# A scan, a sorted mixture of experts and a gated feed-forward on one core: x takes the normalisation's bias ahead of the chain, the down product goes in pieces, and the order tables are new

## The chip, the cores and the metric

The kernel runs on one NeuronCore of a Trainium2 chip. A core has a matrix engine (TensorE, PE in the rows; its weight loads are PEld), a vector engine (VectorE, DVE), an activation engine (ScalarE, ACT), a general engine (GpSimd, POOL) and a queue that mostly starts transfers (SyncE, SP). Each runs its own instruction stream in the order in which it is written; they meet only at semaphores. The metric is the device time of one execution in microseconds (us). Before the change it is 979.82 us, the median of three runs (976.91 to 981.39).

## The reference

The input x is (8, 1024, 128) in f32: 8 sequences of 1024 tokens with 128 features.

```python
def step(h, inps):                                   # over the tokens of a sequence; h is (batch, 128, 16)
    x_t, d_t, B_t, C_t = inps                        # d = softplus(x Wd + bd), B = x WB + bB, C = x WC + bC
    bar_A = jnp.exp(jnp.minimum(d_t[:, :, None] * A, 2.0))           # A = -exp(A_log)
    bar_B = jnp.clip(d_t[:, :, None] * B_t[:, None, :], -2.0, 2.0)
    h = jnp.clip(bar_A * h + bar_B * x_t[:, :, None], -100.0, 100.0)
    return h, jnp.sum(h * C_t[:, None, :], axis=-1) + x_t * D_param
...
routing = softmax(flat @ Wr + br);  top1_w, top1_i = max, argmax     # flat: the scan's outputs, 4 experts
hid = silu(flat @ up_w[e] + up_b[e]);  all_out = hid @ down_w[e] + down_b[e]      # hidden size 512
out = ssm_out + sel * top1_w                                         # sel: the output of the chosen expert
attn = (out - mu) * rsqrt(var + EPS) * ln_w + ln_b
...
x = _layernorm(x + attn)
x = _layernorm(x + (silu(x wg) * (x wu)) wd)         # hidden size 384, weights are integers times 1/127
```

So there are three normalisations over the 128 features: the first (k = 0 in the code) has the weight `ln_w` and the bias `ln_b`, the second (k = 1) follows after x has been added, the third (k = 2) comes after the feed-forward.

## The kernel before, in words

A chunk is one sequence; there are 8. Each is handled whole (1024 tokens, in two halves of 512 where a PSUM bank asks for it, and in 8 tiles of 128 tokens). The stages of a chunk:

- **Inputs of the scan**: TensorE's products z and bc, ScalarE's softplus, VectorE's `delta` (L966) and `dx` (L971), a split of B into three bf16 parts (`bc_rest` on GpSimd L1166, `bc_mid`, `bc_low`), and a bound (`bound_input`, `bound`, `over`, `flag`) which shows whether any clipping can matter; if none can, the scan takes the fast branch.
- **The scan**: 16 states s. For each, ScalarE makes the decay (L758), TensorE spreads row s of B over 128 partitions (`spread`, L519, into psB, one buffer), VectorE multiplies by dx (L1124) and scans in two halves (L1133, three state buffers), GpSimd multiplies by C (`prod`, L1160, three buffers), and TensorE adds the product, turned, into psY (`add`, L525).
- **The router and the sort**: y_copy, turn, logits, then on VectorE `router_shift` (L1004 to L1019), TensorE's `rank`, and VectorE's `slots` (L1037 to L1067). GpSimd scatters the 8 tiles to sorted rows in DRAM (`scatter`, L1181); SyncE reads them back as up to 11 blocks of 128 rows, each with one expert.
- **The experts**: per block a turn (`sort_turn`, `sort_copy`), `up` (L636), `silu` (L796), `down` (L652), `result` (L803), with the block's weights fetched by SyncE (512 KB each, three buffers: block k waits for result k-3). Results go to DRAM (`store`) and come back in token order (`gather` on GpSimd, L1189).
- **The rest**, by halves h: `combine` (VectorE, L1075: chosen output times weight plus y), `stats` k (L1092, L1097), `rstd` k (GpSimd, four tiny instructions L1198 to L1206), `norm` k (ScalarE, L815). Between the first and the second normalisation stands `affine` (GpSimd, L1217 to L1225), three instructions of 128x512: times `ln_w`, plus `ln_b`, plus x. Then x is turned and split in two parts (`x_turn` L661, `x_high`, `x_rest`, `x_low`), six up products `ff_up` (L677, L678), ScalarE's `gate` (L845), VectorE's `ff_mul` (L1104), `ff_down` (L688, L691), the third normalisation, and the output's transfer.

Nothing decides at run time which stage goes next. Five tables (`PE_ORDER`, `ACT_ORDER`, `DVE_ORDER`, `POOL_ORDER`, `SP_ORDER`) each list one round of an engine; an entry `(-1, "up", 3)` means "in round i, task up 3 of chunk i-1". So while chunk n is scanned, the experts of chunk n-1 and the feed-forward of chunk n-2 run beside it. A table can be cut at another point of the round without any change of order, so that only the relative order of entries counts. An engine that waits at one entry holds up all that follow it. The banks U0, U1, D and T of PSUM are counted by fills and drains in the order of `PE_ORDER`.

Since the line numbers move with the change, `affine` is at L1228 and L1234 after it, the products at L1166, the scatters at L1187, the decays at L764, and so on.

## Time and profile before

| what | value |
|---|---|
| runs | 976.91, 979.82, 981.39 us |
| profiled execution, own time | 977.01 us |
| its span, first to last instruction | 975.0 us |
| mean granted clock of TensorE | 0.824 |
| PE / DVE / POOL / ACT busy | 687.9 / 705.7 / 612.3 / 501.3 us |
| a full round (scan 15 to scan 15, chunks 3 to 6) | 102 to 105 us |
| after the last scan (821 to 975) | 154 us |

A timeline row reads: start in us from the span's beginning, duration in us, engine, line, operation, what is written and read, shape, count, and in brackets the idle time before it with what ended that idle time. Busy time on an engine is no proof that the engine sets the pace: with tables like these one reads round by round who waits for whom.

### The profile page before, as it was taken

The numbers are of one execution on the slowest core, as the hardware profiler recorded it, in microseconds if no ns is written. First come the engines' busy times: TensorE is split into PE (matmuls) and PEld (weight loads), VectorE is DVE, ScalarE is ACT, GpSimd is POOL, SyncE is SP. The second block draws the span as 40 slices with busy tenths as digits, with TensorE's granted clock in tenths as the row PEclk, the third lists the DMA queues.
The fourth block names the chain that finished last, engine by engine and source line by source line (L and its number), as shares of the span: only waits on it lengthen the run. The fifth ranks groups of instructions, "written<-read, shape, count | busy, mean of one in ns | idle before, by whom it ended". The sixth has DMA issues, their size and how long they took to land.

```text
span 975.0 us, 14730 instructions
## 1 busy us (share of the span) xinstructions
PE 687.9 (71%) x4648; PEld 549.3 (56%) x4648; DVE 705.7 (72%) x1330; ACT 501.3 (51%) x776; POOL 612.3 (63%) x516
## 2 busy tenths in 40 slices
PE   3465747884899579865997499838985798179244
PEld 1233526762687459743985288626873597158233
DVE  3699999789878988698868977898789764311131
ACT  5563354374664747384739474746643463054222
POOL 0376446468864889388948795689648874550540
PEclk8676877996799779985999599967996699579667
DMA  3333435844485527553765367444845373235100
GB/s 118 108 133 108 144 119 173 278 145 146 144 251 169 189 87 232 198 166 109 239 196 174 124 217 240 145 143 136 262 153 180 108 246 115 89 94 180 41 1 22
DMA packets 82086, 149.17 MB, mean 153 GB/s; under 512 B 9404, under 2 KB 51132, under 8 KB 81992
## 3 DMA queue, kind: packets, MB, share of 16 engines
q1 hardware_dynamic: 69192, 134.97, 42.6%
q0 software_dynamic: 4096, 8.40, 2.6%
q10 hardware_dynamic: 8704, 4.72, 1.8%
q8 instruction: 38, 0.62, 0.3%
q14 instruction: 56, 0.46, 0.2%
HBM read 132.64 MB, written 15.40 MB: 152 GB/s over the span
## 4 chain that ended last, share of the span: by engine, by line
PE 28%; POOL 22%; DVE 19%; issue 16%; ACT 6%; DMA 5%; SPq 1%; POOLq 0%; DVEq 0%; ACTq 0%
DVE state L1133 9%; POOL prod L1160 8%; PE psU L636 5%; DMA weights<-in_w_pack 4%; PE psT L652 4%; POOL rstd L1203 4%; PE psD L691 3%; PE psY L525 3%; DVE moe L1075 3%; POOL rows_in L1181 3%; PE psU L677 2%; DVE psB L1124 2%; PE psB L519 2%; PE psU L678 2%; DVE bst L1092 1%
## 5 line engine op out<-in xcount | busy, mean ns | idle before, releaser
L1160 POOL TENSOR_TENSOR prod<-state,c_wide 128x1024 f32<-128x1024 f32 x128 | 312.2, 2444 | 174.6 <-DVE state L1133 156.9
L519 PE MATMUL psB<-parts,sel 128*128 128x512 bf16 x256 | 110.4, 447 | 146.1 <-DVE state L1133 141.8
L1124 DVE TENSOR_TENSOR psB<-dx,psB 128x512 f32<-128x512 f32 x256 | 167.4, 689 | 34.3 <-PE psB L519 26.3
L1133 DVE TENSOR_TENSOR_SCAN state<-decay,state,psB 128x512 f32<-128x512 f32 x128 | 163.8, 1280 | 14.4 <-DVE state L1133 0.5
L525 PE MATMUL psY<-ident,prod 128*128 128x128 f32 x1024 | 157.9, 308 | 12.4 <-POOL prod L1160 12.4
L1133 DVE TENSOR_TENSOR_SCAN state<-decay,psB 128x512 f32<-128x512 f32 x128 | 155.2, 1213 | 5.1 <-ACT decay L758 4.8
L758 ACT ACTIVATE decay<-delta,a_sb 128x1024 f32<-128x1024 f32 x128 | 140.5, 1141 | 32.8 <-DVE state L1133 27.0
L525 PEld LDWEIGHTS psY<-ident,prod 128*128 128x128 f32 x1024 | 137.5, 160 | 28.7 <-POOL prod L1160 17.1
L519 PEld LDWEIGHTS psB<-parts,sel 128*128 128x128 bf16 x256 | 25.7, 103 | 201.5 <-DVE state L1133 190.3
L636 PE MATMUL psU<-yT_sorted,weights 128*128 128x128 f32 x704 | 126.0, 300 | 8.8 <-DMA weights<-in_w_pack 8.0
L636 PEld LDWEIGHTS psU<-yT_sorted,weights 128*128 128x128 f32 x704 | 111.0, 195 | 17.2 <-DMA weights<-in_w_pack 10.6
L796 ACT ACTIVATE hid<-psU 128x512 f32<-128x512 f32 x88 | 52.3, 594 | 103.3 <-PE psU L638 101.2
L652 PE MATMUL psT<-weights,hid 128*128 128x128 f32 x704 | 97.6, 282 | 0.0
L652 PEld LDWEIGHTS psT<-weights,hid 128*128 128x128 f32 x704 | 85.8, 192 | 1.3
L1181 POOL DMA_INDIRECT rows_in<-ytok,slot x64 | 66.7, 1043 | 30.8 <-issue 26.8
L1104 DVE SCALAR_TENSOR_TENSOR hh<-psU,hh 128x512 f32<-128x512 f32 x48 | 32.4, 689 | 70.9 <-PE psU L678 70.6
L638 PE MATMUL psU<-of_block,bias 96*128 96x128 bf16 x352 | 78.5, 223 | 0.0
L1189 POOL DMA_INDIRECT chosen_out<-rows_out,slot x64 | 61.7, 964 | 23.0 <-issue 14.6
L815 ACT ACTIVATE attn<-attn,shift,rstd 128x128 f32<-128x128 f32 x64 | 26.3, 482 | 70.1 <-POOL shift L1206 70.1
L815 ACT ACTIVATE moe<-moe,shift,rstd 128x128 f32<-128x128 f32 x64 | 26.3, 482 | 63.5 <-POOL shift L1206 63.0
L691 PE MATMUL psD<-wdn_sb,hh 128*128 128x128 f32 x384 | 53.3, 275 | 0.0
L1203 POOL TENSOR_TENSOR rstd<-ve,minus_half 128x4 f32<-128x4 f32 x48 | 49.2, 1025 | 3.8
(153 smaller groups left out, 1150.7 us busy)
## 6 DMA issues: line engine op xcount, KB each, us to landing
c_wide<-c_rows SPq DMA_DIRECT2D x128, 512.0 KB
weights<-in_w_pack SPq DMA_DIRECT2D x88, 512.0 KB, 4.7
xT_sb<-in_xT SPq DMA_DIRECT2D x8, 512.0 KB, 3.6
y_sorted<-rows_in SPq DMA_DIRECT2D x16, 256.0 KB, 3.0
xt<-in_x SPq DMA_DIRECT2D x8, 512.0 KB, 4.7
rows_out<-result SPq DMA_DIRECT2D x16, 256.0 KB, 5.5
out<-x ACTq DMA_DIRECT2D x16, 256.0 KB, 4.0
y_sorted<-rows_in SPq DMA_DIRECT2D x8, 192.0 KB, 4.8
```

The costliest lines, as they stand in the source:

```text
L519: pe.matmul(tokens(psB, c, h), sel[:, s, :], parts[:, c.n % 2, h * HALF:h * HALF + c.hw], start=True, stop=True).then_inc(b_ready, 1)
L525: mm = pe.matmul(psY[:, j, :], src[:, j * ROWS:(j + 1) * ROWS], ident[:, :], is_transpose=True, start=(first and j % NJ == 0), stop=last, ...
L636: pe.matmul(bank[u][:, cols], weights[:, q % NW, f * 128:(f + 1) * 128], yT_sorted[:, k * ROWS:(k + 1) * ROWS], start=(f == 0), stop=False ...
L638: mm = pe.matmul(bank[u][:, cols], bias3[:, f * 128:(f + 1) * 128], of_block[:, n % 2, k:k + 1].to_broadcast([96, ROWS]), start=False, sto ...
L652: mm = pe.matmul(bank[d][:, 0:D], hid[:, k % 2, f, :], weights[:, q % NW, W_DOWN + f * D:W_DOWN + (f + 1) * D], start=False, stop=(f == NF ...
L691: mm = pe.matmul(bank["D"][:, cols], hh[:, m, cols], wdn_sb[:, m, :], start=False, stop=(m == NH - 1), skip_group_check=True)
L758: nc.scalar.activation(decay[:, g % NDECAY, w], delta[:, n % 2, w], ACT.Exp, scale=a_sb[:, s:s + 1]).then_inc(decay_ready, 1)
L1124: v.tensor_tensor(tokens(psB, c, h), dx[:, n % 2, h * HALF:h * HALF + c.hw], tokens(psB, c, h), ALU.mult).then_inc(inp_ready, 1)
L1133: v.tensor_tensor_scan(state[:, g % NSTATE, t0:t0 + c.hw], decay[:, g % NDECAY, t0:t0 + c.hw], tokens(psB, c, h), before, ALU.mult, ALU.ad ...
L1160: g_.tensor_tensor(prod[:, g % NPROD, w], state[:, g % NSTATE, w], c_wide[:, g % NC, w], ALU.mult).then_inc(prod_ready, 1)
L1181: g_.indirect_dma_start(rows_in, bass.IndirectOffsetOnAxis(slot[:, n % 2, j:j + 1].bitcast(U32), 0), ytok[:, n % 2, j, :], None).then_inc( ...
L1203: g_.tensor_tensor(rstd[:, h, hj], ve[:, h, hj], minus_half[:, hj], ALU.pow).then_inc(rstd_steps, 1)
```

## The change

Four edits:

1. `affine` loses its middle instruction. A new task `x_shift` on GpSimd adds `ln_b` to x in place, as soon as x has come in; `affine` is then times `ln_w`, plus the shifted x. The semaphore counts go from 3 to 2 a turn, and `affine` waits for `shifted`.
2. `ff_down` keeps only the products with the identity (x into the bank); three new tasks `ff_part h m` add the hidden parts m = 0, 1, 2, each with its own wait for its `ff_mul`. Before, one task waited for all three and went tile by tile.
3. New tables for all five engines.
4. The tables are cut at other points of the round (which by itself moves nothing).

```diff
 PE_ORDER = [
...
+    (-1, "up", 3), (-2, "ff_down", 0), (-2, "ff_part", 0, 0), (-2, "ff_part", 0, 1), (-2, "ff_part", 0, 2),
...
 DVE_ORDER = [
-    (0, "router_shift"), (1, "scan", 3), (1, "scan", 4), (0, "slots"), (-1, "combine", 0), (-1, "stats", 0, 0),
+    (1, "scan", 2), (0, "router_shift"), (1, "scan", 3), (0, "slots"), (-1, "combine", 0), (-1, "stats", 0, 0),
...
 SP_ORDER = [
-    (-1, "c", 12), (-2, "weights", 5), (-1, "c", 13), (-2, "weights", 6), (-1, "c", 14), (-2, "weights", 7),
+    (-3, "weights", 5), (-3, "weights", 6), (-2, "c", 13), (-3, "weights", 7), (-2, "c", 14), (-3, "weights", 8),
...
+            def add_ff(c, h, m):
+                u = f"U{(m + NH) % 2}"
+                pe.wait_ge(drained[u], fills(u, c, ("ff_up", h, m + NH)))
+                for j in range(c.hj):
+                    cols = slice(j * 128, (j + 1) * 128)
+                    mm = pe.matmul(bank["D"][:, cols], hh[:, m, cols], wdn_sb[:, m, :], start=False,
+                                   stop=(m == NH - 1), skip_group_check=True)
+                if m == NH - 1:
+                    mm.then_inc(filled["D"], 1)
...
                 if name == "ff_down":
                     (h,) = args
-                    for m in range(NH):
-                        u = f"U{(m + NH) % 2}"
-                        pe.wait_ge(drained[u], fills(u, c, ("ff_up", h, m + NH)))
                     fill("D", c, task)
                     for j in range(c.hj):
-                        cols = slice(j * 128, (j + 1) * 128)
-                        pe.matmul(bank["D"][:, cols], ident127[:, :], attn[:, h * NJ + j, :], start=(j == 0), stop=False,
-                                  skip_group_check=True)
-                        for m in range(NH):
-                            mm = pe.matmul(bank["D"][:, cols], hh[:, m, cols], wdn_sb[:, m, :], start=False,
-                                           stop=(m == NH - 1), skip_group_check=True)
-                    mm.then_inc(filled["D"], 1)
+                        pe.matmul(bank["D"][:, j * 128:(j + 1) * 128], ident127[:, :], attn[:, h * NJ + j, :],
+                                  start=(j == 0), stop=False, skip_group_check=True)
...
+                if name == "x_shift":
+                    (h,) = args
+                    jj = slice(h * NJ, h * NJ + c.hj)
+                    if n == 0 and h == 0:
+                        pool.wait_ge(consts_in, 16 * LATE)
+                    pool.wait_ge(xt_in, 16 * (n + 1))
+                    lb = lnb_sb[:, :].rearrange("p (o d) -> p o d", o=1).to_broadcast([128, c.hj, D])
+                    g_.tensor_tensor(xt[:, jj, :], xt[:, jj, :], lb, ALU.add).then_inc(shifted[h], 1)
                 if name == "affine":
...
                     g_.tensor_tensor(moe[:, jj, :], moe[:, jj, :], lw, ALU.mult).then_inc(affine_steps[h], 1)
-                    pool.wait_ge(affine_steps[h], 3 * turn + 1)
-                    g_.tensor_tensor(moe[:, jj, :], moe[:, jj, :], lb, ALU.add).then_inc(affine_steps[h], 1)
-                    pool.wait_ge(affine_steps[h], 3 * turn + 2)
-                    pool.wait_ge(xt_in, 16 * (n + 1))
+                    pool.wait_ge(affine_steps[h], 2 * turn + 1)
+                    pool.wait_ge(shifted[h], turn + 1)
```

What the new tables move, at three places. First GpSimd, from the product of scan 3 to that of scan 4 and beyond, with the first normalisation of half 0 (`ve` to `shift` is `rstd 0 0`). Before:

```order
L1160 TENSOR_TENSOR prod<-state,c_wide 128x1024
L1181 DMA rows_in<-ytok,slot 1408x128
L1160 TENSOR_TENSOR prod<-state,c_wide 128x1024
L1198 TENSOR_TENSOR ve<-mv,eps 128x4
L1200 TENSOR_TENSOR minus_mean<-mv,minus_one 128x4
L1203 TENSOR_TENSOR rstd<-ve,minus_half 128x4
L1205 ISA
L1206 TENSOR_TENSOR shift<-minus_mean,rstd 128x4
L1181 DMA rows_in<-ytok,slot 1408x128
L1217 TENSOR_TENSOR moe<-moe,lnw_sb 128x512
L1219 TENSOR_TENSOR moe<-moe,lnb_sb 128x512
L1225 TENSOR_TENSOR attn<-moe,xt 128x512
```

With the change:

```order
L1166 TENSOR_TENSOR prod<-state,c_wide 128x1024
L1204 TENSOR_TENSOR ve<-mv,eps 128x4
L1206 TENSOR_TENSOR minus_mean<-mv,minus_one 128x4
L1209 TENSOR_TENSOR rstd<-ve,minus_half 128x4
L1211 ISA
L1212 TENSOR_TENSOR shift<-minus_mean,rstd 128x4
L1221 TENSOR_TENSOR xt<-xt,lnb_sb 128x512
L1187 DMA rows_in<-ytok,slot 1408x128
L1166 TENSOR_TENSOR prod<-state,c_wide 128x1024
L1228 TENSOR_TENSOR moe<-moe,lnw_sb 128x512
L1234 TENSOR_TENSOR attn<-moe,xt 128x512
L1195 DMA chosen_out<-rows_out,slot 128x128
```

The reciprocal deviation now comes before the product of scan 4, the shift of x and a scatter stand between it and `affine`, and one gather has moved behind `affine`.

Second, GpSimd from the last six scatters on. Before:

```order
L1181 DMA rows_in<-ytok,slot 1408x128 x6
L1160 TENSOR_TENSOR prod<-state,c_wide 128x1024
L1166 TENSOR_TENSOR bnd<-bcf,parts 128x1024
L1198 TENSOR_TENSOR ve<-mv,eps 128x4
L1200 TENSOR_TENSOR minus_mean<-mv,minus_one 128x4
L1203 TENSOR_TENSOR rstd<-ve,minus_half 128x4
L1205 ISA
L1206 TENSOR_TENSOR shift<-minus_mean,rstd 128x4
L1160 TENSOR_TENSOR prod<-state,c_wide 128x1024
L1217 TENSOR_TENSOR moe<-moe,lnw_sb 128x512
```

With the change:

```order
L1187 DMA rows_in<-ytok,slot 1408x128 x6
L1221 TENSOR_TENSOR xt<-xt,lnb_sb 128x512
L1204 TENSOR_TENSOR ve<-mv,eps 128x4
L1206 TENSOR_TENSOR minus_mean<-mv,minus_one 128x4
L1209 TENSOR_TENSOR rstd<-ve,minus_half 128x4
L1211 ISA
L1212 TENSOR_TENSOR shift<-minus_mean,rstd 128x4
L1166 TENSOR_TENSOR prod<-state,c_wide 128x1024 x2
L1172 TENSOR_TENSOR bnd<-bcf,parts 128x1024
```

The product of scan 6 (`prod`, the first after the scatters) now stands behind the second shift of x and behind `rstd 1 0`; `bc_rest` (`bnd<-bcf,parts`) stands one product later.

Third, ScalarE from the split of x (`x1h`, `x1l`) to the first expert blocks (`ex` is the router's exponential, `hh` the gates, `yT_sorted` is `sort_copy 0`, `hid` is `silu`). Before:

```order
L832 ACTIVATE x1h<-psD 128x512
L758 ACTIVATE decay<-delta,a_sb 128x1024
L838 ACTIVATE x1l<-psD 128x512
L758 ACTIVATE decay<-delta,a_sb 128x1024
L780 ACTIVATE ex<-rs 128x32
L845 ACT_TABLE_LOAD
L845 ACTIVATE hh<-psU 128x512 x3
L787 ACTIVATE yT_sorted<-psD 128x512
L815 ACTIVATE moe<-moe,shift,rstd 128x128 x4
L796 ACTIVATE hid<-psU 128x512
```

With the change:

```order
L838 ACTIVATE x1h<-psD 128x512
L844 ACTIVATE x1l<-psD 128x512
L764 ACTIVATE decay<-delta,a_sb 128x1024
L851 ACT_TABLE_LOAD
L851 ACTIVATE hh<-psU 128x512 x3
L786 ACT_TABLE_LOAD
L786 ACTIVATE ex<-rs 128x32
L821 ACTIVATE moe<-moe,shift,rstd 128x128 x4
L764 ACTIVATE decay<-delta,a_sb 128x1024
L793 ACTIVATE yT_sorted<-psD 128x512
L802 ACT_TABLE_LOAD
L802 ACTIVATE hid<-psU 128x512 x2
```

The exponential has gone behind the gates, the normalisation `moe` (`norm 1 0`) and one decay ahead of `sort_copy 0`, and there are two more table loads. Over the whole kernel ScalarE has 58 table loads in place of 46.

Moves that are told in words: on VectorE `slots`, `combine 0` and `stats 0 0` come after scan 3 instead of scan 4, `router_pick` from after scan 1 to between the `ff_mul` of half 0, `delta` from behind scan 8 and `stats 1 0` to right behind scan 7, ahead of `combine 1`, `dx` from after scan 13 to after scan 12, `stats 1 1` and `stats 0 2` together after scan 11. On TensorE `yT_turn` comes right after z and ahead of the spread of scan 2, `up 3` ahead of `ff_down 0`, `down 8` behind the spread of scan 15. On SyncE weights 6 and 7 each move ahead of one load of C, the stores 0 and 1 after the next round's first load of C, and `over` behind weights 10. On ScalarE the third normalisation `norm 1 2` goes ahead of `y_copy`.

## Rows read from the trace of the kernel before

**Rows 1.** the page: span, and busy time of each engine with its share
```profile
span 975.0 us, 14730 instructions
...
PE 687.9 (71%) x4648; PEld 549.3 (56%) x4648; DVE 705.7 (72%) x1330; ACT 501.3 (51%) x776; POOL 612.3 (63%) x516
```

**Rows 2.** stretches: length; PE, PEld, DVE, ACT, POOL busy us; granted clock, DMA, GB/s
```profile
513.20:617.00 103.80, 83.26 (x595) 68.13 (x594) 85.47 (x164) 63.86 (x99) 78.81 (x65) 0.87 0.56 180
...
821.00:975.00 154.00, 79.15 (x506) 63.48 (x505) 30.55 (x145) 48.05 (x105) 59.78 (x85) 0.74 0.23 71
...
534.00:563.00 29.00, 14.84 (x52) 9.55 (x53) 26.29 (x62) 15.20 (x22) 23.69 (x23) 0.53 0.34 117
...
563.00:616.00 53.00, 50.02 (x409) 44.77 (x408) 40.49 (x75) 29.04 (x52) 37.63 (x31) 1.00 0.67 210
```

**Rows 3.** timeline, VectorE: start, us, instruction, [idle before]; flag of two chunks
```profile
301.00 0.64 DVE L994 TENSOR_REDUCE clip_flag<-over_row 1x1 int32<-1x512 f32 x1
...
714.92 0.64 DVE L994 TENSOR_REDUCE clip_flag<-over_row 1x1 int32<-1x512 f32 x1
```

**Rows 4.** timeline, VectorE then GpSimd: the two combines, and a product beside the first
```profile
536.03 4.14 DVE L1075 SCALAR_TENSOR_TENSOR moe<-chosen_out,top_w,ytok 128x128 f32<-128x128 f32 x4
...
554.34 1.12 DVE L1075 SCALAR_TENSOR_TENSOR moe<-chosen_out,top_w,ytok 128x128 f32<-128x128 f32 x4
...
537.66 2.35 POOL L1160 TENSOR_TENSOR prod<-state,c_wide 128x1024 f32<-128x1024 f32 x1
```

**Rows 5.** one line's instructions, VectorE: ns min/median/max; a timeline row of the second
```profile
L1075 DVE SCALAR_TENSOR_TENSOR moe<-chosen_out,top_w,ytok x64: 322/346/3261, 223.8 to 930.4; 128x128 f32<-128x128 f32 x64
...
L966 DVE SCALAR_TENSOR_TENSOR delta<-zb,sp x8: 1192/1212/7559, 16.9 to 663.6; 128x1024 f32<-128x1024 f32 x8
...
663.57 6.13 DVE L966 SCALAR_TENSOR_TENSOR delta<-zb,sp 128x1024 f32<-128x1024 f32 x1
```

**Rows 6.** groups by line, GpSimd; then its timeline at the scatters
```profile
L1219 POOL TENSOR_TENSOR moe<-moe,lnb_sb 128x512 f32<-128x512 f32 x16 | 20.3, 1270 | 1.3
...
560.42 1.97 POOL L1181 DMA_INDIRECT rows_in<-ytok,slot  x1 [0.30 <-issue]
...
562.42 2.39 POOL L1160 TENSOR_TENSOR prod<-state,c_wide 128x1024 f32<-128x1024 f32 x1
```

**Rows 7.** timeline, ScalarE then TensorE: second normalisation, first expert block
```profile
553.39 1.65 ACT L815 ACTIVATE attn<-attn,shift,rstd 128x128 f32<-128x128 f32 x4 [7.15 <-POOL shift L1206]
...
566.49 0.66 PE L624 MATMUL psD<-ident,y_sorted 128*128 128x128 f32 x4 [1.18 <-DMA y_sorted<-rows_in]
...
567.92 0.46 PE L636 MATMUL psU<-yT_sorted,weights 128*128 128x128 f32 x2
```

**Rows 8.** timeline, VectorE: its waits in a round
```profile
571.23 0.69 DVE L1124 TENSOR_TENSOR psB<-dx,psB 128x512 f32<-128x512 f32 x1 [1.24 <-POOL prod L1160]
...
599.71 0.06 DVE L984 MEMSET holder<- 128x1 f32 x1 [4.07 <-PE psT L580]
...
628.07 0.19 DVE L1004 TENSOR_TENSOR rs<-psT,br_sb 128x32 f32<-128x32 f32 x1 [0.69 <-PE psT L597]
```

**Rows 9.** timeline, TensorE: the wait for weights in the dense stretch
```profile
597.70 0.49 PE L636 MATMUL psU<-yT_sorted,weights 128*128 128x128 f32 x2 [0.86 <-DMA weights<-in_w_pack]
```

**Rows 10.** groups by line, ScalarE: table loads ahead of the decays
```profile
L758 ACT ACT_TABLE_LOAD x21 | 26.9, 1283 | 2.3 <-ACT yT_sorted L787 1.1 <-ACT result L803 1.0
```

**Rows 11.** timeline of the end: GpSimd, then VectorE
```profile
844.80 1.05 POOL L1181 DMA_INDIRECT rows_in<-ytok,slot  x1 [3.12 <-issue]
...
920.78 0.21 POOL L1198 TENSOR_TENSOR ve<-mv,eps 128x4 f32<-128x4 f32 x1
...
922.42 0.20 POOL L1206 TENSOR_TENSOR shift<-minus_mean,rstd 128x4 f32<-128x4 f32 x1 [0.17 <-POOL rstd L1203]
...
961.67 1.53 DVE L1104 SCALAR_TENSOR_TENSOR hh<-psU,hh 128x512 f32<-128x512 f32 x2 [0.42 <-PE psU L678]
...
967.30 0.89 DVE L1092 BATCH_NORM_STATS2 bst<-psD 128x6 f32<-128x128 f32 x4 [4.10 <-PE psD L691]
```

More of the change, by code:

```diff
@@ L87 @@
+    (1, "spread", 1, 0), (1, "spread", 1, 1), (0, "add", 15), (2, "z"),
 ]
 ACT_ORDER = [
-    (-2, "result", 7), (-2, "silu", 8), (-2, "silu", 9), (-2, "result", 8), (-2, "silu", 10), (-2, "result", 9),
-    (0, "decay", 0), (-2, "result", 10), (0, "decay", 1), (0, "decay", 2), (0, "decay", 3), (-1, "y_copy"),
-    (-3, "norm", 1, 2), (-1, "yT_copy"), (0, "decay", 4), (1, "z_copy"), (1, "softplus"), (1, "bc_copy"),
-    (0, "decay", 5), (0, "decay", 6), (0, "decay", 7), (0, "decay", 8), (0, "decay", 9), (-2, "norm", 0, 0),
@@ L101 @@
+    (-1, "result", 2), (-1, "sort_copy", 2), (-1, "silu", 3), (0, "decay", 13), (0, "decay", 14), (0, "decay", 15),
+    (-2, "norm", 1, 1), (-1, "result", 3), (-1, "silu", 4), (-2, "norm", 0, 2), (-1, "result", 4), (-2, "x_high", 1),
+    (-1, "silu", 5), (-1, "silu", 6), (-2, "x_low", 1), (-1, "result", 5), (-2, "gate", 1, 0), (-2, "gate", 1, 1),
+    (-1, "result", 6),
 ]
 DVE_ORDER = [
-    (-2, "stats", 1, 0), (1, "delta"), (-2, "ff_mul", 0, 0), (-2, "ff_mul", 0, 1), (-2, "ff_mul", 0, 2),
@@ L123 @@
[L123 to L127 removed]
+    (-2, "c", 10), (-3, "weights", 3), (-3, "x"), (-2, "c", 11), (-3, "weights", 4), (-2, "c", 12),
@@ L179, in exists @@
         return task[1] < c.tiles
-    if name in ("x_turn", "x_rest", "x_high", "x_low", "ff_up", "gate", "ff_mul", "ff_down", "norm", "stats", "rstd",
-                "affine", "combine", "b_spread", "bound"):
+    if name in ("x_turn", "x_rest", "x_high", "x_low", "ff_up", "gate", "ff_mul", "ff_down", "ff_part", "norm", "stats", "rstd",
+                "affine", "x_shift", "combine", "b_spread", "bound"):
         return task[1] < c.halves
```

96 lines of the change are left out of this document (46 added, 50 removed), and 3 rows, old and new, of the table SP_ORDER.

## The prediction

> **What bounds the kernel now.** I read the engines' busy time first [rows 1], then the stretches [rows 2], the timelines of one round, and last the end of the span. The first view shows no engine that bounds: VectorE is busy 705.7 of 975.0 us, TensorE 687.9. The stretches show why an average misleads. A full round of 103.8 us has VectorE at 85 and TensorE at 83, but they take turns: from 534 to 563 VectorE works 26.3 of 29 us and TensorE 14.8, from 563 to 616 TensorE works 50.0 of 53 and VectorE 40.5. So a round is a loop with a front, paced by VectorE and GpSimd (router, slots, combine, first and second normalisation, scatters), and a dense stretch paced by TensorE. The last 154 us have neither: VectorE 30.6, TensorE 79.2, a chain of latencies. Rounds: the clip flag is read at 301.00 and at 714.92, four chunks later [rows 3], 413.9 us or 103.5 a round.
>
> In the front the reader is to see two stalls. The first `combine` takes 4.14 us, the second 1.12 with the same four instructions; a GpSimd product runs from 537.66 to 540.01 beside the first [rows 4]. The dense stretch starts when the sorted rows are there: the turn at 566.49 waited 1.18 us for them, and the first expert block goes at 567.92 [rows 7]. From then on VectorE is the one that waits: 4.07 us at 599.71 for TensorE, 1.24 at 571.23 for a product [rows 8].
>
> **The change part by part.** The sum is against the profiled execution (span 975.0, own time 977.0 us); the median of the three runs, 979.8, is 2.8 above it and I add that at the end.
>
> *The front of a round.* (a) The router: `router_pick` leaves its place (two instructions, 0.4 us), the turn of y no longer stands behind a spread that waits for scan 1, and VectorE's wait of 0.69 at 628.07 [rows 8] goes; together -0.9. (b) `slots` and `combine 0` come one scan earlier: a scan is about 3.85 us on VectorE; the rank products, which need the router, may then be 0.4 late. So `combine 0` starts at about 536.0 - 0.9 - 3.85 + 0.4 = 531.7 on this round's scale. (c) GpSimd is then issuing gathers, and its product of scan 3 comes after them, so that the combine should take 1.12, not 4.14: 3.0 of VectorE's work saved. (d) But GpSimd must finish that product before `rstd 0 0` (about 535.0, with one gather fewer ahead of it). From there: rstd 1.84 (920.78 to 922.62 [rows 11]) to 536.9; `norm 0 0` 1.65 beside `x_shift` (1.27 [rows 6]); a scatter, the product of scan 4 and two instead of three steps of `affine`, to 544.3. VectorE needs three scans and the statistics after its own, to 547.1, and sets the next step: second normalisation at 549.1 in place of 553.39 [rows 7], -4.3.
>
> (e) What is late next is GpSimd again. Product 5 and six scatters with one delay of 1.0 us by `delta` (today the last scatter takes 1.97 [rows 6]) end at about 560.0, against 562.4. Then the new table puts `x_shift 1` and `rstd 1 0` (1.27 + 1.84 = 3.1) before the product of scan 6, which today starts at 562.42 [rows 6]: now 563.1, 0.7 late. And ScalarE has `norm 1 0` (1.65) and a decay (1.15) ahead of `sort_copy 0`: 563.1 + 1.65 + 1.15 + 0.6 = 566.5, and the first expert block at 566.6 against 567.92 [rows 7]: -1.3. So most of the 4.3 is eaten.
>
> *The dense stretch.* The same matmuls run, at 50 busy of 53 us. The wait for weights, 0.86 [rows 9], goes: weights 7 no longer stand behind a load of C that waits for product 11, and need only result 4. `down 8` (0.95) goes behind the last spread and comes back before the next round's decay 0. Net -0.9. The pieces of the down product gain nothing here: TensorE does not wait at it, they are cover for `ff_mul 1 2`, which now stands behind scan 14. ScalarE gets two more table loads of 1.283 us a round [rows 10]: the one at `silu 0` falls while the first block's products run, the one at the exponential delays `router_pick` and with it `ff_mul 0 1` by some 1.2 us, while VectorE would else wait for the product of scan 6: nothing. x's load, behind `affine`, gets 2.6 us later and has 9 us until its next user. Per round -1.3 - 0.9 = -2.2, bounds 0 and -4.3. Six rounds feel it (chunks 2 to 7): **-13**.
>
> *The lock.* `delta` takes 1.21 as a median, 7.56 at most [rows 5]; three of eight take over 6 (7.56, 6.08, and the 6.13 whose row stands there). The long ones meet products on GpSimd that follow each other with no gap. Right behind scan 7 it meets at most one product and then scatters. Two of the long ones lie in the rounds counted; 4.9 us each on VectorE, of which TensorE's slack hides about half: **-5**, bounds 0 and -10. The Trainium skill (SBUF — State Buffer, Who interferes with whom) says that a VectorE instruction with two SBUF inputs and a GpSimd instruction that reads SBUF exclude each other, and that whoever issues first holds the pair for the whole instruction. For the combine the trace agrees: its longest is 3261 ns, one product and something [rows 5]. For `delta` it does not: 7559 is more than one product (2.35) can explain. By the page alone `dx`, which moves into GpSimd's row of products behind scan 12, could lose 2.4 us at most; by the row 6.4.
>
> *The end.* Every step here is on the chain. Up to the second normalisation of chunk 6: `norm 1 2` no longer between `y_copy` and the turn -1.1, one step of `affine` -1.35, the scatter before it -1.1, and its wait of 3.12 [rows 11], of which I can't say whether it follows the scatter or the place (half: -1.5); a gather and a scatter before `rstd 0 1` cost 0.8. Sum -4.3, from -2.7 to -5.9; it passes on to the experts of chunk 7, since scatters and x both come earlier. For chunk 7: `rstd 0 0` starts with the statistics and not behind the eighth gather (920.78 [rows 11]) -0.9; two halves of `affine`, -1.35 each, in one chain. The last down product: today the last `ff_mul` ends at 963.20, and the statistics start at 967.30 after a wait of 4.10 for TensorE [rows 11]. In pieces only four of sixteen matmuls (some 0.9 to 1.1) follow the last `ff_mul`: -2.9. Sum -4.3 - 0.9 - 2.7 - 2.9: **-10.8**, from -8 to -14.
>
> Total: -13 - 5 - 10.8 = -28.8; 977.0 becomes 948.2, and the median 979.8 becomes 951.0.
>
> **Rivals.**
>
> *The rounds keep their length* (only the end gains). For: (e) shows GpSimd giving back 3.1 of 4.3, and `dx` blocked for 6.4 in each round against a cover of 4.07 [rows 8] costs 2.3 x 6 = 14, the whole term. Against: `dx` precedes scan 13, which waits for a product anyway. 979.8 - 10.8 - about 2 = 967.
>
> *The dense stretch starts later* (slower). Place: GpSimd after the scatters. If these don't come earlier (gathers or the combine late by 2.4), product 6 ends 3.1 later than today, and scan 9, which needs it, starts at 567.9, where now its products start at 566.0: +1.9 a round, 11.4 in six. With an end that gains only 5.6 (affine and pieces) the time is 986. It decides once the last scatter ends less than 1.2 us earlier than today, since then scan 9 is later than now. For: the order has it so. Against: the combine's 3.0 us must fail to come back.
>
> *The clock.* TensorE was granted 0.53 in 534 to 563, where it worked half the time, and 1.00 in 563 to 616 [rows 2]: 1.2 and 2.4 GHz. If the changed waits leave ten more microseconds of dense work at the lower level, that costs 5 a round, 30 in all, and the time is 981. For: more bits of work now stand in the front. Against: the dense stretch keeps its fill.
>
> **How the numbers follow.** Forecast 0.62, its own range 939 to 964 (rounds -4 to -1, lock -10 to 0, end -14 to -8). Rounds keep their length 0.18, later dense stretch 0.12, clock 0.08. What a measurement can tell here is about 0.5%, 975 to 984.7. Faster: 0.62 + 0.16 + 0.02 = 0.80; same: 0.02 + 0.02 + 0.04 = 0.08; slower: 0.10 + 0.02 = 0.12. The range of 938 to 974 leaves out the slower rival, most of the clock's and a small part of the forecast below 938.
>
> **What would show it.** In the changed profile: `combine 0` at 1.1 to 1.3 us in every round; no `delta` over 4 us; rounds of 100 to 101.5 by the flag; product 6 right behind `rstd 1 0`; `affine` in two rows of 1.27; the last statistics 1.1 to 1.4 us behind the last `ff_mul`; the stretch after the last scan at 143 us. Wrong it is if rounds stay at 103 or more, if `combine 0` still takes 4, or if the end stays above 150.

## The result and the profile after

The changed kernel takes 966.4 us (median of 964.96, 965.91, 966.89 and 968.84) against 978.4 for the kernel before in the same job: a ratio of 0.9873, 95% interval 0.9842 to 0.9904, or 12 us faster. Forecast were 951.0, 28.8 us faster. The direction was right; the size was less than half. The time lies in the range (938 to 974) and on the number of the rival "the rounds keep their length" (967), by luck, as is shown below. Of the six executions of `n_all_prod3` below the profiled one was slow, so that its ratio leaves it out and nothing is read from its trace.

The profiled execution took 964.96 us. The page, and the stretches at the same places as in [rows 2] (5.6 us earlier, as the round starts; the last one from the end of the last scan, 6.2 earlier):

```profile
span 962.8 us, 14646 instructions
...
PE 681.2 (71%) x4589; PEld 547.8 (57%) x4648; DVE 694.4 (72%) x1330; ACT 519.7 (54%) x788; POOL 613.8 (64%) x516
```
```profile
507.60:611.40 103.80, 82.81 (x575) 67.22 (x582) 85.45 (x164) 65.60 (x99) 77.25 (x65) 0.85 0.52 177
814.80:962.80 148.00, 79.12 (x516) 64.00 (x514) 31.57 (x145) 48.65 (x105) 59.97 (x85) 0.74 0.23 74
528.40:557.40 29.00, 17.83 (x57) 10.37 (x56) 26.91 (x64) 15.02 (x22) 22.09 (x23) 0.56 0.44 148
557.40:610.40 53.00, 49.55 (x401) 44.33 (x406) 39.68 (x74) 31.36 (x55) 37.85 (x31) 0.99 0.61 209
```

VectorE has 11 us less to do in the whole span, and not a microsecond less in this round (85.45 against 85.47), in which the change was to save it 3. The granted clock in the two parts of this round is that of before, 0.56 and 0.99 against 0.53 and 1.00, so that the rival of the clock is out for the rounds. The stretch after the last scan went from 154.0 to 148.0, and the flags (compare [rows 3]) give 708.38 - 293.56 = 414.8, or 103.7 a round where before had 103.5:

```profile
293.56 0.67 DVE L1000 TENSOR_REDUCE clip_flag<-over_row 1x1 int32<-1x512 f32 x1 [0.50 <-DMA over_row<-over]
...
708.38 0.67 DVE L1000 TENSOR_REDUCE clip_flag<-over_row 1x1 int32<-1x512 f32 x1 [1.57 <-DMA over_row<-over]
```

So one of the signs of being wrong is there, rounds at 103 or more. That mean hides two things, which the starts of each chunk's first scan separate (us, chunks 0 to 6): before 70.2, 95.4, 106.4, 103.7, 102.2, 102.6, 105.5; after 69.6, 93.2, 102.9, 103.1, 103.4, 103.8, 103.5. Chunks 1, 2 and 6, in which `delta` was caught for 6 to 7.6 us, got 2.2, 3.5 and 2.0 shorter. Chunks 4 and 5, in which it was not, got 1.2 **longer**. (Chunk 3, right behind a caught one, got 0.6 shorter; with `delta` alone moved, in `f_delta_early` below, it is 102.4, so that it too got longer by all the rest of the change.)

Where the saved 3.0 us of the combine went is seen in the timeline of VectorE and GpSimd (compare [rows 4]); the rows of the second block are one line's instructions each, ns min/median/max, and its first row is of the kernel before:

```profile
520.63 2.90 DVE L1025 TENSOR_TENSOR chosen<-rcode,rsmall 128x32 bf16<-128x32 f32 x1
...
529.60 1.14 DVE L1081 SCALAR_TENSOR_TENSOR moe<-chosen_out,top_w,ytok 128x128 f32<-128x128 f32 x4
...
521.12 2.35 POOL L1166 TENSOR_TENSOR prod<-state,c_wide 128x1024 f32<-128x1024 f32 x1
```
```profile
L1019 DVE TENSOR_TENSOR chosen<-rcode,rsmall x8: 191/192/193, 126.5 to 833.8; 128x32 bf16<-128x32 f32 x8
...
L1025 DVE TENSOR_TENSOR chosen<-rcode,rsmall x8: 191/2898/3043, 125.9 to 825.9; 128x32 bf16<-128x32 f32 x8
...
L1081 DVE SCALAR_TENSOR_TENSOR moe<-chosen_out,top_w,ytok x64: 337/344/1352, 220.0 to 922.2; 128x128 f32<-128x128 f32 x64
...
L972 DVE SCALAR_TENSOR_TENSOR delta<-zb,sp x8: 1200/1331/1660, 16.9 to 652.9; 128x1024 f32<-128x1024 f32 x8
```

The combine takes 1.14, as forecast, and `delta` is never long. But `chosen`, the router's last instruction in `router_shift`, of 0.19 us before in all eight chunks, now takes 2.64 to 3.04 in six of them: the product of scan 2 stands beside it, and `chosen` ends 0.06 us behind it. The table has this product between gathers 3 and 4, where before it came behind gather 5.

What follows it in the round: second normalisation, last scatter, product 6 and the first expert block (compare [rows 6, 7]), and VectorE at scan 9 (compare [rows 8]):

```profile
547.27 1.65 ACT L821 ACTIVATE attn<-attn,shift,rstd 128x128 f32<-128x128 f32 x4 [9.39 <-POOL shift L1212]
...
556.97 0.97 POOL L1187 DMA_INDIRECT rows_in<-ytok,slot  x1 [0.30 <-issue]
557.96 1.29 POOL L1221 TENSOR_TENSOR xt<-xt,lnb_sb 128x512 f32<-128x512 f32 x1
...
561.00 2.36 POOL L1166 TENSOR_TENSOR prod<-state,c_wide 128x1024 f32<-128x1024 f32 x1
...
562.09 0.66 PE L638 MATMUL psD<-ident,y_sorted 128*128 128x128 f32 x4 [1.39 <-DMA y_sorted<-rows_in]
563.41 1.09 PE L527 MATMUL psY<-ident,prod 128*128 128x128 f32 x8 [0.66 <-POOL prod L1166]
564.39 0.46 PE L650 MATMUL psU<-yT_sorted,weights 128*128 128x128 f32 x2
...
563.60 1.29 DVE L1130 TENSOR_TENSOR psB<-dx,psB 128x512 f32<-128x512 f32 x2 [2.95 <-POOL prod L1166]
```

Counted from the round's first scan (508.78; before 514.35): second normalisation 38.5 (39.0), last scatter's end 49.2 (48.0), start of product 6 52.2 (48.1), first expert block 55.6 (53.6). From there to the next chunk's first scan it is 48.2 (49.0). So in this round the front is 2.0 longer, the dense stretch 0.8 shorter.

### The profile page after: what moved, and what is told of

Read it like the earlier page. It is cut to its first block, busy times and chain, and to the rows that moved or that the text cites. A ratio compares the mean times of both kernels' runs of the same rounds, so it can differ in the third digit from the quotient of the medians.

```text
span 962.8 us, 14646 instructions
## 1 busy us (share of the span) xinstructions
PE 681.2 (71%) x4589; PEld 547.8 (57%) x4648; DVE 694.4 (72%) x1330; ACT 519.7 (54%) x788; POOL 613.8 (64%) x516
## 4 chain that ended last, share of the span: by engine, by line
PE 35%; DVE 23%; issue 16%; POOL 14%; DMA 6%; ACT 5%; SPq 1%; another core or an unknown queue 1%; DVEq 0%; ACTq 0%; POOLq 0%
DVE state L1139 11%; PE psU L650 8%; PE psT L666 6%; POOL rows_in L1187 4%; PE psD L551 4%; DVE psB L1130 4%; PE psY L527 3%; POOL prod L1166 3%; PE psB L521 2%; POOL rstd L1209 2%; PE psU L576 2%; DVE bst L1098 2%; DMA weights<-in_w_pack 2%; PE psU L652 2%; PE psU L691 1%
## 5 line engine op out<-in xcount | busy, mean ns | idle before, releaser
L521 PE MATMUL psB<-parts,sel 128*128 128x512 bf16 x197 | 85.6, 457 | 126.6 <-DVE state L1139 122.0
L527 PE MATMUL psY<-ident,prod 128*128 128x128 f32 x1024 | 151.9, 300 | 6.0 <-POOL prod L1166 3.6
L764 ACT ACTIVATE decay<-delta,a_sb 128x1024 f32<-128x1024 f32 x128 | 142.6, 1141 | 20.7 <-DVE state L1139 13.8
L650 PEld LDWEIGHTS psU<-yT_sorted,weights 128*128 128x128 f32 x704 | 109.3, 195 | 10.8 <-DMA weights<-in_w_pack 3.9
L802 ACT ACTIVATE hid<-psU 128x512 f32<-128x512 f32 x88 | 52.3, 598 | 85.1 <-PE psU L652 84.0
L1204 POOL TENSOR_TENSOR ve<-mv,eps 128x4 f32<-128x4 f32 x48 | 9.8, 204 | 91.3 <-DVE mv L1103 90.8
L675 PE MATMUL psD<-ident,attn 128*128 128x128 f32 x64 | 14.2, 363 | 75.4 <-ACT attn L821 69.0
L809 ACT ACTIVATE result<-psT 128x128 f32<-128x128 f32 x88 | 24.3, 276 | 63.6 <-PE psT L666 61.0
```

Of the source, the lines that this page charges most:

```text
L521: pe.matmul(tokens(psB, c, h), sel[:, s, :], parts[:, c.n % 2, h * HALF:h * HALF + c.hw], start=True, stop=True).then_inc(b_ready, 1)
L527: mm = pe.matmul(psY[:, j, :], src[:, j * ROWS:(j + 1) * ROWS], ident[:, :], is_transpose=True, start=(first and j % NJ == 0), stop=last, ...
L650: pe.matmul(bank[u][:, cols], weights[:, q % NW, f * 128:(f + 1) * 128], yT_sorted[:, k * ROWS:(k + 1) * ROWS], start=(f == 0), stop=False ...
L764: nc.scalar.activation(decay[:, g % NDECAY, w], delta[:, n % 2, w], ACT.Exp, scale=a_sb[:, s:s + 1]).then_inc(decay_ready, 1)
L802: nc.scalar.activation(hid[:, k % 2, :, :], bank[u][:, :].rearrange("p (f r) -> p f r", f=NF), ACT.Silu).then_inc(drained[u], 1)
```

## The experiments

A time is given with its ratio to the kernel before, run in the same job. "The lock" is what the prediction calls the mutual exclusion of a VectorE instruction with two SBUF inputs and a GpSimd instruction that reads SBUF. Theory 1 is that it moved to `chosen`; theory 2, that GpSimd's row behind the scatters sets the round; theory 3, that ScalarE's order does. Offsets are us from the round's first scan, in the round of chunk 5 if nothing else is said. In the expectations H is `h_router_gather7` and G `g_act_order`.

**Run a_router_psum.** The lock's two inputs:

```diff
-v.tensor_reduce(rsmall[:, 1, j], rcode[:, j, :], X, ALU.max)
-v.tensor_tensor(chosen[:, j, :], rcode[:, j, :], wide(rsmall[:, 1, j], c.tiles, E), ALU.is_equal)
+v.tensor_reduce(top_code, rcode[:, j, :], X, ALU.max)          # top_code: eight columns of bank T, in PSUM
+v.tensor_tensor(chosen[:, j, :], rcode[:, j, :], wide(top_code, c.tiles, E), ALU.is_equal)
```
(the first maximum, `rsmall[:, 0, j]`, likewise)

> The changed kernel; in router_shift the two small maxima are kept in PSUM, so that `chosen` no longer has two SBUF inputs. Theory 1 (the lock only moved, from the first combine to `chosen`): `chosen` takes 0.2 to 0.4 us instead of 2.90 in every round, the first combine starts 2.2 us earlier (0.6 stays as the wait for the rank products), the rounds get 2.2 shorter, 966.4 - 6 x 2.2 = 953. Theory 1b: the lock goes on to the next instruction that stands beside a product; the combine then starts at about 20.8 - 2.9 = 18 us into the round, where the product of scan 3 starts (18.5), takes 3 to 4 us again, and the time stays at 964 to 968. Theory 2 (GpSimd's row behind the scatters sets the round): the front comes earlier by at most the 4.0 us that GpSimd waits in it, and scan 9 keeps its wait of about 3 us.

962.1 us, 0.9849 [0.9823, 0.9875]. Timeline of VectorE and GpSimd:

```profile
520.36 0.19 DVE L1026 TENSOR_TENSOR chosen<-rcode,psT 128x32 bf16<-128x32 f32 x1
520.84 2.35 POOL L1167 TENSOR_TENSOR prod<-state,c_wide 128x1024 f32<-128x1024 f32 x1
...
526.01 3.88 DVE L1082 SCALAR_TENSOR_TENSOR moe<-chosen_out,top_w,ytok 128x128 f32<-128x128 f32 x4
526.84 2.37 POOL L1167 TENSOR_TENSOR prod<-state,c_wide 128x1024 f32<-128x1024 f32 x1
```

The mechanism of theory 1b; the time is 2 us under its 964 to 968. With one input in PSUM `chosen` takes 0.19 just ahead of the same product, so it was the lock. The combine then comes 3.3 us earlier, meets the product of scan 3 and takes 3.88. The statistics end 0.5 earlier, and a round is 0.4 shorter (mean of chunks 3 to 6).

**Run h_router_gather7.** The same, and in `POOL_ORDER`:

```diff
-(-2, "gather", 6), (0, "prod", 3), ... (-2, "affine", 0), (-2, "gather", 7),
+(-2, "gather", 6), (-2, "gather", 7), (0, "prod", 3), ... (-2, "affine", 0),
```

> The kernel with the router's maxima in PSUM, and gather 7 put ahead of product 3 on GpSimd, so that the first combine (17.5 us into the round) stands beside gathers. Theory 1 (one collision of a product with VectorE's two-input work is left whatever is moved, until the product itself is moved): the combine takes 1.14 at 17.5, statistics 18.7, product 3 is done at 22.1, rstd 0 0 then, second normalisation at 35.3 us instead of 37.8, last scatter 45.8 instead of 48.3, first expert block 52.3 instead of 54.9: rounds 101, and 962.1 - 6 x 2.5 = 947. Rival: the dense stretch's length grows by what the front gives (as when product 6 and the copy were put first, where the block came 1.0 earlier and the round kept its length): 960 to 962.

953.0 us, 0.9754 [0.9728, 0.9779].

```profile
518.55 1.14 DVE L1082 SCALAR_TENSOR_TENSOR moe<-chosen_out,top_w,ytok 128x128 f32<-128x128 f32 x4
...
520.63 2.36 POOL L1167 TENSOR_TENSOR prod<-state,c_wide 128x1024 f32<-128x1024 f32 x1
...
620.52 3.17 DVE L1082 SCALAR_TENSOR_TENSOR moe<-chosen_out,top_w,ytok 128x128 f32<-128x128 f32 x1
...
621.17 2.36 POOL L1167 TENSOR_TENSOR prod<-state,c_wide 128x1024 f32<-128x1024 f32 x1
```

With both collisions gone the round does what the forecast said of it: second normalisation at 35.2 (after: 38.5), last scatter's end 45.9 (49.2), first expert block 52.3 (55.6), rounds of chunks 2 to 5 at 99.9, 100.1, 99.8 and 100.5. The rival, that the dense stretch takes it back, falls. Chunk 6 kept 103.3; its rows are the last two: there the combine came 0.7 later in the round, and its fourth instruction was caught again. That is 3 of the 6 us by which 953 misses 947; another 1.5 lie in chunk 0, which took 71.3 instead of 69.8, and the rest I have not followed.

**Run b_prod6_first** and **run c_both_first.** `POOL_ORDER`: `(0, "prod", 6)` ahead of `(-2, "x_shift", 1), (-2, "rstd", 1, 0)`; in the second also `ACT_ORDER`: `(-1, "sort_copy", 0)` ahead of `(-2, "norm", 1, 0), (0, "decay", 12)`.

> The changed kernel with product 6 put back ahead of x_shift 1 and rstd 1 0 on GpSimd; nothing else. Theory 2: scan 9's wait of 2.95 us goes, scan 9 starts 2.5 to 3 us earlier in each round. But rstd 1 0 is then 2.4 later, and ScalarE has norm 1 0 and a decay ahead of the copy of the sorted rows, so the first expert block goes 1.5 to 2 us later: 966.4 + 0 to 12, that is 966 to 978. If the expert block were bound by product 6 alone, it would come 1 us earlier and the time would be 960. Theory 1 (lock at `chosen`): no change of the front, 966.

985.3 us, 1.0084 [1.0059, 1.0109].

> As the run before it, and on ScalarE the copy of the sorted rows ahead of norm 1 0 and decay 12. Theory 2: the first expert block 1.0 us earlier than in the changed kernel (then bound by the sorted rows, 562.1 in the round shown, and the copy), scan 9 3 us earlier: rounds 1 to 2 us shorter, 966.4 - 6 to -12 = 954 to 960. Theory 1: the front is late by `chosen`, so that the last scatter and the sorted rows are where they are; no more than 1 us a round, 960 at best. Rival (TensorE's 50 us of work in the dense stretch bounds, whatever the front does): 966.

966.9 us, 0.9899 [0.9874, 0.9923].

The first is 19 us slower than the changed kernel, where 0 to 12 were expected, and slower than before the change: rstd 1 0 is later, and on ScalarE `norm 1 0` holds the copy of the sorted rows until 57.1 (after: 54.9), with rounds of 105 to 109. The first expert block is 2.2 later, as expected; that the rounds grew by 2 to 6 is more than that, and stays open. In the second the copy is at 53.9, the first expert block 1.0 earlier, scan 9 3.2 earlier and right behind `ff_mul`, without a wait. Yet rounds are 103.0 to 103.9, and the time is the rival's 966. TensorE has a new wait:

```profile
570.30 0.22 PE L663 MATMUL psT<-bias,of_block 96*128 96x128 bf16 x1 [1.04 <-ACT hid L802]
```

It waits for `silu 0`, which stands behind `norm 1 0`, decay 12 and a table load. So theory 2 alone falls: taking away the 2.95 us that VectorE waited at scan 9 gained nothing.

**Run g_act_order.** The second of these, with `decay 12` and `router_exp` ahead of the three gates and `norm 1 0` behind `silu 0` in `ACT_ORDER`.

> The kernel with product 6 and the copy of the sorted rows put first; on ScalarE also decay 12 and the router's exponential ahead of the three gates (two table loads fewer a round) and norm 1 0 behind silu 0. Theory 3 (ScalarE took back what product 6 and the copy gave: TensorE waited 1.04 us for silu 0): that wait goes, the first expert block stays at 54.3 to 54.6, rounds of 102 to 102.5, 966.9 - 6 to -9 = 958 to 961. Rival (TensorE's own work from the first expert block on, 48.1 us and a wait of 0.75, has grown by something else): 966.

961.8 us, 0.9844 [0.9819, 0.9870]. 5 less than without ScalarE's part, just above the 958 to 961 expected; but the rounds of chunks 3 to 6 are 103.0 to 103.7 by the profile, where 102 to 102.5 were, and what is gained against `c_both_first` lies in chunks 1, 2 and 7 (1.6, 1.1 and 2.8). So ScalarE's order is worth some 5 us, but not 1 in every round, and theory 3 has nearly the size, but not the place.

**Run r_prod5_early.** `POOL_ORDER`: `(0, "prod", 5)` ahead of `(-2, "rstd", 0, 1)`, as it was before the change.

> The changed kernel with product 5 ahead of rstd 0 1 on GpSimd, where before the change it stood. GpSimd waits 1.42 us there for the statistics, so product 5 costs rstd 0 1 only 0.94, and the six scatters start 1.4 us earlier. If the last scatter bounds the dense stretch: last scatter 47.7 instead of 49.1, rounds 1.4 shorter, 966.4 - 6 x 1.4 = 958. Rival: the second normalisation, 0.94 later, moves the gated network's up products and with them norm 1 0 and the copy of the sorted rows by as much: 966 to 972.

960.2 us, 0.9818 [0.9781, 0.9855]: last scatter at 47.2 (49.2), first expert block 54.2 (55.6), rounds of chunks 2 to 6 at 102.1 to 102.7, 1.0 shorter in the mean, though the second normalisation is 0.8 later (39.3). So much the new place of product 5 costs, apart from the lock.

**Run d_code_only**, **run f_delta_early**, **run q_code_delta.** The change in parts, on the tables of before: the code's edits alone (x_shift ahead of each affine, parts behind `ff_down`); `delta` alone; both.

```diff
-(-2, "stats", 1, 0), (1, "delta"), (-2, "ff_mul", 0, 0), ...
+(-2, "stats", 1, 0), (-2, "ff_mul", 0, 0), ... (1, "scan", 7), (2, "delta"), (-1, "combine", 1),
```

> The tables of before with the three edits of the code: x_shift right ahead of each affine, affine in two steps, the down product's parts right behind ff_down. Both theories: the end gains two affine halves (x_shift runs in the wait for norm), 2 x 1.35, and the 1.05 us that TensorE waited for the last ff_mul, 3.7 to 4 together; the rounds keep their length, so about 978.4 - 4 = 974.5. If the edits of the code also shorten the rounds (1.35 less before the second normalisation's statistics, of which scans hide part), -1 a round, 968; then the new order gave next to nothing.

973.1 us, 0.9958 [0.9938, 0.9978].

> The kernel before with one edit: delta of the chunk after next right behind scan 7, where the new table has it. The three long delta (7.56, 6.08, 6.13) become 1.2 to 1.7. Forecast's term: -5. By the lengths of the two traces' rounds (chunk 1 -2.2, chunk 2 -3.5, chunk 6 -2.0): -7.7, so 978 - 7.7 = 970. Rival (the stalls hide behind TensorE's work, and delta now delays scan 8 by 1.7 in each round): 976 to 980.

971.7 us, 0.9954 [0.9922, 0.9985]; of its `delta` (ns min/median/max):

```profile
L967 DVE SCALAR_TENSOR_TENSOR delta<-zb,sp x8: 1198/1201/1770, 17.0 to 651.8; 128x1024 f32<-128x1024 f32 x8
```

> The tables of before, the three edits of the code, and delta behind scan 7; nothing else of the new order. If the change is worth these two alone (-4.6 and -6.2 in the runs by themselves): 977.8 - 10.8 = 967.0, the changed kernel's time, and the rest of the new order is worth nothing. If the new front gives something that a loss hides (my forecast gave it -13): 972 or more.

967.5 us, 0.9892 [0.9853, 0.9931], as expected. In the trace of `f_delta_early` the rounds of chunks 2 to 6 take 102.6 in the mean; in the changed kernel 103.4. So against the kernel with `delta` alone moved, all the rest of the change makes each of these rounds 0.7 longer. That the changed kernel is faster than `f_delta_early` all the same comes mostly from its end and from the round of chunk 7, the last: from its first scan to the end of its last one that takes 102.3 in `f_delta_early` (98.4 before, 98.7 after). There the router waits 2.94 for TensorE and another of its instructions is caught:

```profile
728.22 0.19 DVE L1005 TENSOR_TENSOR rs<-psT,br_sb 128x32 f32<-128x32 f32 x1 [2.94 <-PE psT L598]
...
728.74 3.02 DVE L1010 TENSOR_TENSOR rs<-rs,rsmall 128x32 f32<-128x32 f32 x1
...
729.34 2.36 POOL L1161 TENSOR_TENSOR prod<-state,c_wide 128x1024 f32<-128x1024 f32 x1
```

By the ratios the edits of the code are worth 4.1 us, `delta` 4.5, both 10.6, the whole change 12.4, each within 2 to 4. The rest of the new order, nearly all of the diff, gives the 1.8 between the last two, which is less than their uncertainty.

**Run e_tables_only** and **run p_no_pieces.** The new tables on the old code; and the changed kernel with one edit, which makes the down product wait for all three `ff_mul`:

```diff
 if name == "ff_down":
     (h,) = args
+    for m in range(NH):
+        u = f"U{(m + NH) % 2}"
+        pe.wait_ge(drained[u], fills(u, c, ("ff_up", h, m + NH)))
     fill("D", c, task)
```

> The new tables on the code of before: affine in three steps, no x_shift, the down product in one piece. Against the changed kernel the end loses 2 x 1.35 for affine and 1.05 for the last down product, 3.8. In the rounds GpSimd has affine 0 1.35 longer ahead of the second normalisation (which waited 1.4 for VectorE: hidden), and no x_shift 1 (1.27) ahead of product 6, which comes 1.3 earlier; in the dense stretch the unsplit down product waits for ff_mul 1 2 behind scan 14, 0 to 1 us. If product 6 bounds the first expert block: rounds -0.7, so 966.4 + 3.8 - 4 + 0 to 6 = 966 to 972. If the cost of the new tables is elsewhere: 970 to 976.

991.2 us, 1.0145 [1.0117, 1.0173].

> The changed kernel, but the down product waits for all three ff_mul before its first matmul, as before the change. Forecast's view (the parts gain nothing in a round, they cover ff_mul 1 2 behind scan 14): a cover that is gone costs. From the run with the new tables on the old code (rounds of 106.8 against 103.4): TensorE waits at ff_down 1 for ff_mul 1 2 behind scan 14, about 3 us in each of six or seven rounds, and 1.05 at the end: 966.4 + 19 to 22 = 985 to 988. Rival (the 3 us came from affine's third step or the missing x_shift): 967.5.

997.0 us, 1.0192 [1.0157, 1.0228].

```profile
622.13 1.13 PE L701 MATMUL psD<-attn,ident 128*128 128x128 f32 x8 [2.58 <-DVE hh L1113]
```

Scan 15, whose spread stands behind the down product on TensorE, starts 102.7 us into the round instead of 98.5 (mean of chunks 3 to 6), and rounds are 106.4 to 109.2. So the pieces carry 3 to 6 us in each round of this order, since `ff_mul 1 2` stands behind scan 14 and would hold TensorE. The wait itself is 2.6 to 3.0 in each round, the 3 that I had expected; why three of them grew by 5 to 6 I don't know. For the tables alone I had 966 to 976, since there I put this wait at 0 to 1.

**Runs k_all, n_all_prod3, s_all_prod5, t_all_prod3b.** What the experiments point to: the first is `h_router_gather7` with the moves of `g_act_order`; the others move one product more in `POOL_ORDER`: product 3 behind `x_shift 0`; product 5 ahead of `rstd 0 1`; product 3 between `rstd 0 0` and `x_shift 0`.

> The router's maxima in PSUM, gather 7 ahead of product 3, product 6 ahead of x_shift 1 and rstd 1 0, the copy of the sorted rows, decay 12 and the router's exponential early, norm 1 0 behind silu 0. If the front (H: 953.0) and the start of the dense stretch (G: -4.6 against the changed kernel) add up: 953.0 - 4.6 = 948.4; scan 9's wait of 2.94 goes. If a round of 100 is bound elsewhere by now (VectorE is busy 85, TensorE 83): 952 to 953.

948.9 us, 0.9693 [0.9657, 0.9729], the forecast 948.4 met. A round of it:

```profile
508.00:607.00 99.00, 79.87 (x568) 65.50 (x576) 82.74 (x162) 62.22 (x97) 76.43 (x65) 0.88 0.55 185
```

> As the run before it, with product 3 behind rstd 0 0 and x_shift 0. The combine then stands beside gathers in every round, also in the round of chunk 6, where it took 3.97 in H and the round 103.3: that round -3; in the others rstd 0 0 starts 1.9 earlier, but GpSimd waited only 0.95 us between there and its last scatter, so at most -0.9 each: 948.4 - 3 - 0 to 5 = 941 to 945. If add 3, which waits for the product, holds up the spreads of scans 6 and 7 on TensorE: 948 to 952.

954.4 us, 0.9751 [0.9713, 0.9788]: slower than `k_all`, and above both ranges. Whether the late add 3 is the cause I leave open.

> The fastest kernel so far (948.9) with the same move of product 5. GpSimd waits about 1 us at rstd 0 1 there. If the last scatter bounds: 948.9 - 6 = 943. Rival as above: 949 to 955.

954.6 us, 0.9773 [0.9727, 0.9819]. What helped the changed kernel harms this one: the second normalisation is 1.8 later (37.5 against 35.7 in the mean of chunks 3 to 6), and the first expert block with it, though the last scatter in chunks 3 to 5 isn't. In `k_all` GpSimd waits only 0.55 us at `rstd 0 1`, where the changed kernel waits 1.42, and a product takes 2.35: what is put ahead of it makes it late.

> The fastest kernel so far with product 3 right behind rstd 0 0 and ahead of x_shift 0. The combine then takes 1.14 in chunk 6's round too (-3 there). Product 3 comes 2.3 later than in the fastest kernel, 1.3 earlier than in the run with it behind x_shift 0 (954.4), and add 3 with the spreads behind it 2.3 later: if that lateness is what cost 5.5 there, 948 to 952; if only the second normalisation counts (rstd 0 0 earlier by 1.9): 944.

948.2 us, 0.9707 [0.9667, 0.9747]. The combine takes 1.14 in chunk 6's round too, and the round is 100.9 instead of 102.7, but chunk 2's is 101.7 instead of 99.9: the same time as `k_all`. These two beat both kernels of this case, by 3% and 1.8%.

## Why the prediction was wrong

**The step that failed is "the front of a round", (a) to (e): the first expert block was to start 1.3 us earlier, and starts 2.0 later** (2.2 later than in `f_delta_early`, mean of chunks 3 to 6). With the 0.9 of the dense stretch it stood in the sum as -2.2 a round, -13 for six. Beyond what `f_delta_early` has, the last scan ends 2.0 earlier, and none of that is in the rounds of chunks 2 to 6, which are 0.7 longer each. In its parts:

- (a), (b), (c): the combine was to start 4.35 earlier and to take 1.12. It took 1.14 and started 0.9 earlier: of the 3.0 saved, 2.7 were lost 9 us ahead of it, at `chosen`. I had looked for the products that stand beside the instruction that was slow before, and not for what the moved product now stands beside. With both collisions removed (`h_router_gather7`) the combine starts 4.2 earlier, the second normalisation 3.8 (forecast 4.3) and the first expert block 1.3 (forecast 1.3) than before the change, so that the arithmetic held and the neighbours did not.
- (d), (e): with -4.3 at the second normalisation the last scatter was to come 2.4 earlier. With -0.5 it came 1.1 later. Without the two collisions, in `h_router_gather7`, it comes 2.2 earlier than before the change, with product 5 where the new table has it: so they are 3.3 of the 3.5 between forecast and result. With them, product 5 in its old place gives 1.1 of it back (`r_prod5_early`, mean of chunks 3 to 6).
- The rival "the dense stretch starts later" named this mechanism, its place and its price: from a last scatter less than 1.2 earlier on, 1.9 us a round. The first expert block starts 2.0 later. I gave it 0.12 because "the combine's 3.0 us must fail to come back", which is just what happened. Its 986 took +1.9 in all six rounds and put the lock and the gain of the dense stretch at nothing; these came (the next two terms), and only the rounds of chunks 4 and 5 grew against before.
- Its reason, though, was that scan 9 waits for product 6. `c_both_first` removes the wait and gains nothing, so scan 9 is not what sets the round.
- The rival "the rounds keep their length" has the time, 967, by luck. Its reason was `dx` blocked for 6.4; no `dx` took over 2.43. It had 10.8 from the end and about 2 from the rest, where 6.2 and 6.0 came.

**The dense stretch**, forecast -0.9 for the wait for weights and `down 8`: 49.0 to 48.2, right.

**The lock**, -5: `f_delta_early` gives -4.5 [-1.5, -7.6], and no `delta` is over 1.66 in the changed kernel. Right in the mechanism; the size is in part luck, since in the traces the rounds of chunks 1 to 6 gain 8.2 and chunk 7's loses 3.9, with the wait and the catch shown above.

**The table loads**, forecast free: there are 58 instead of 46. `g_act_order` takes them out again and moves two tasks besides, for 5 us together; I have not separated these, so that this step stays open.

**The pieces** in a round, forecast as cover that gains nothing: right, and `p_no_pieces` shows what is under it, 30 us.

**The end**, forecast -10.8, measured -6.2 (154.2 to 148.0 behind the last scan), each against the last scan's end:

| step | forecast | measured |
|---|---|---|
| up to chunk 6's second normalisation | -4.3 | -2.5 |
| the same at the last expert block of chunk 7 | -4.3 | -1.6 |
| rstd 0 0, first half of affine | -2.25 | -2.2 |
| second half of affine | -1.35 | -1.2 |
| last down product | -2.9 | -1.3 |

The first row: `norm 0 0` starts 0.3 earlier (forecast 1.1), `affine` ends another 3.1 earlier (forecast 4.0, with the half of the 3.12), and gather and scatter take 0.9 back (0.8).

The second row: chunk 7's experts start 3.3 us earlier and take 1.7 longer. For 3.3 us of their first blocks TensorE is granted 0.50, which is 1.2 GHz (a stretch; then a matmul ahead of it and the same one in it, and last the same one of the kernel before):

```profile
859.10:862.40 3.30, 3.30 (x19) 2.99 (x17) 1.25 (x8) 0.86 (x2) 1.72 (x4) 0.50 0.00 0
```
```profile
858.46 0.44 PE L650 MATMUL psU<-yT_sorted,weights 128*128 128x128 f32 x2
...
859.16 0.74 PE L650 MATMUL psU<-yT_sorted,weights 128*128 128x128 f32 x2
...
867.98 0.44 PE L636 MATMUL psU<-yT_sorted,weights 128*128 128x128 f32 x2
```

Five such pairs start 0.64 us apart instead of 0.34, which makes 1.5 of the 1.7. Before the change the pairs of these blocks took 0.39 to 0.46. Ahead of the first block TensorE idled 0.78 in both traces. In the 6 us ahead of that it idled another 0.75 in the trace of after (858.11 is the block's start) and 1.51 in that of before; why only one of them fell back I can't tell. This is read from the rows, and no run tests it.

The last row: I let only four of sixteen matmuls follow the last `ff_mul`. The rows (compare [rows 11]; the first one is of the kernel before) show all three parts behind it:

```profile
963.45 0.46 PE L688 MATMUL psD<-attn,ident 128*128 128x128 f32 x2 [1.05 <-DVE hh L1104]
...
950.93 0.54 PE L692 MATMUL psU<-x1l,wu_sb 128*128 128x512 f32 x1
951.31 1.05 PE L698 MATMUL psD<-attn,ident 128*128 128x128 f32 x8
952.20 2.84 PE L551 MATMUL psD<-wdn_sb,hh 128*128 128x128 f32 x24
...
951.58 0.69 DVE L1110 SCALAR_TENSOR_TENSOR hh<-psU,hh 128x512 f32<-128x512 f32 x1 [0.24 <-PE psU L692]
...
955.09 0.89 DVE L1098 BATCH_NORM_STATS2 bst<-psD 128x6 f32<-128x128 f32 x4 [2.81 <-PE psD L551]
```

TensorE itself was busy with the last up products until 951.47. From then on it has 3.6 us of work, and the last `ff_mul` is done 0.8 us into it. The pieces could save the 1.05 us in which it waited for `ff_mul` in the trace of before, and hardly more: what a change saves on a busy engine can't be larger than that engine's idle time, and I had taken VectorE's (4.10, [rows 11]).

## What to carry to other kernels

When a table moves an instruction out of a collision, list for every long instruction of the other engine what stands beside it in the new order, not only what became of the old pair: here the 3 us moved twice, to `chosen` and back to the combine, until a gather filled the place. When one of two engines that alternate is freed, ask which others have slack in that stretch: product 5 on GpSimd took back 1.0 us a round, ScalarE's order some 5 us in all. And a piece of code that gains next to nothing in the rounds of the old order (the pieces: in the trace of before TensorE waits at most 0.15 us at a down product there) may be what the new order stands on: take the parts out one by one, and both with and without the rest.
